# Context weights of tiles 2 and 3 through two free banks, and two wide products ahead of the context sums

## What is computed

```python
scores = jnp.einsum('bhqd,bhkd->bhqk', q, k) / np.sqrt(DK)   # k, v from the 120 context rows
attn = jax.nn.softmax(scores + causal, axis=-1)
out = jnp.einsum('bhqk,bhkd->bhqd', attn, v)
return out @ Wp.T + bp
```

## Time and profile before

| what | value |
|---|---|
| median of 3 runs | 1305.82 us (1305.32 to 1306.38) |
| the profiled execution's own time | 1306.38 us |
| its span in the trace | 1304.6 us |
| period 2, from its first head turn | about 950 to 1070 us |
| period 3 | about 1071 to 1181 us |
| mean granted TensorE clock | 0.947 |

### The profile page before, as it was taken

The page is one execution under the profiler, slowest core; times in us unless marked ns, Lnnn a source line. Parts: engine busy times, 40 slices in busy tenths (PEclk is TensorE's granted clock), DMA queues, the critical chain, the costliest instruction groups (busy, mean ns, idle before and its releaser), DMA issues. The chain is left out here.

```text
span 1304.6 us, 20364 instructions
## 1 busy us (share of the span) xinstructions
PE 1129.9 (87%) x6738; PEld 794.6 (61%) x6738; DVE 744.8 (57%) x2247; ACT 540.8 (41%) x1407; POOL 454.8 (35%) x531
## 2 busy tenths in 40 slices
PE   7889988998898887799999937686998899789996
PEld 3456446545654565799999924452654575466775
DVE  1472476347525835465556528765749576856356
ACT  1371255126422721333333227364465456443541
POOL 0150034004300667566666441525031512222122
PEclk9999999998999997799999958688998999899999
DMA  5000200020001040741111150101000100000000
GB/s 192 17 1 1 56 17 2 1 56 17 1 1 56 2 159 17 262 144 50 50 49 47 40 173 1 33 1 33 1 8 1 33 10 17 1 1 25 1 1 33
DMA packets 40228, 52.38 MB, mean 40 GB/s; under 512 B 10780, under 2 KB 33372, under 8 KB 40124
## 3 DMA queue, kind: packets, MB, share of 16 engines
q1 hardware_dynamic: 31100, 36.66, 8.8%
q0 software_dynamic: 3408, 9.31, 2.6%
q10 hardware_dynamic: 5616, 5.11, 1.2%
HBM read 41.76 MB, written 9.31 MB: 39 GB/s over the span
## 5 line engine op out<-in xcount | busy, mean ns | idle before, releaser
L1327 PE MATMUL bank<-words 128*128 128x256 f32 (+3 forms) x872 | 279.1, 472 | 33.7 <-ACT words L1878 17.4
L1327 PEld LDWEIGHTS bank<-words 128*128 128x128 f32 (+1 forms) x872 | 166.1, 198 | 120.6 <-issue 60.7
L358 PE MATMUL bank<-words 128*128 128x512 f32 x384 | 172.4, 600 | 8.4 <-DMA words<-in_wq 8.4
L324 POOL TENSOR_TENSOR words<-words 128x256 f32<-128x256 f32 (+1 forms) x128 | 103.5, 829 | 192.1 <-DVE words L700 192.1
L886 PEld LDWEIGHTS bank<-words 128*128 128x128 f32 x1248 | 147.7, 195 | 4.2 <-ACT words L920 2.3
L886 PE MATMUL bank<-words 128*128 128x128 f32 x1248 | 148.2, 278 | 1.6 <-ACT words L920 1.6
L571 ACT ACTIVATE words<-words 128x128 f32<-128x128 f32 (+1 forms) x256 | 113.3, 444 | 52.3 <-DVE words L695 52.3
L358 PEld LDWEIGHTS bank<-words 128*128 128x128 f32 x384 | 72.3, 192 | 90.2 <-issue 89.6
L553 ACT ACTIVATE words<-bank 128x512 f32<-128x512 f32 x48 | 28.7, 597 | 191.9 <-PE bank L358 191.9
L935 ACT ACTIVATE words<-words 128x1024 f32 x39 | 41.2, 1057 | 146.5 <-PE bank L886 124.5
L610 DVE COPY words<-bank 128x512 f32<-128x512 f32 x48 | 33.2, 691 | 105.5 <-PE bank L358 105.3
(11 more groups left out here) (300 smaller groups left out, 1991.3 us busy)
## 6 DMA issues: line engine op xcount, KB each, us to landing
words<-in_w SPq DMA_DIRECT2D x8, 1024.0 KB, 12.0
y_slots<-words ACTq DMA_DIRECT2D x39, 128.0 KB, 1.8
words<-in_w SPq DMA_DIRECT2D x8, 512.0 KB, 12.3
words<-in_xt SPq DMA_DIRECT2D x4, 512.0 KB, 4.0
words<-in_x SPq DMA_DIRECT2D x4, 512.0 KB, 4.3
x_rows<-words SPq DMA_DIRECT2D x16, 128.0 KB, 1.8
words<-in_wm SPq DMA_DIRECT2D x2, 1024.0 KB, 6.8
out_x<-words SPq DMA_DIRECT2D x16, 128.0 KB, 1.8
```

The costliest lines, as they stand in the source:

```text
L324: last = pool.tensor_tensor(part, part, inv[:, j % SLOTS0, :, t:t + 1].to_broadcast([P, 2, P * (t + 1)]), ALU.mult)
L358: last = pe.matmul(bank[c % 2][:, :], w, r, start=k == 0, stop=k == KD - 1)
L1327: last = pe.matmul(out, w, r, start=i == 0, stop=i == len(pairs) - 1)
```

## The change

In periods 2 and 3 the turned weights of tiles 2 and 3 go to banks 6 and 7, no longer to bank 1. The fourth `queries_keys`, which uses bank 1, waits for the first two copies alone and stands ahead of those two turns. `up` 0 and 1, which stood between the context sums, stand ahead of all four sums. ACT's order stays; its copies of tiles 2 and 3 read the other banks. The numbers of instructions stay as they were, and period 1 and the closing part issue what they did before.

```diff
@@ tensor, for p in range(1, PERIODS) @@
                 if z is not None:
-                    context_turn(z, 2)
-                    context_turn(z, 3)
-                    pe.wait_ge(xtc, NT * z + NT)
+                    pe.wait_ge(xtc, NT * z + HALF)
                 if a is not None:
                     queries_keys(a, 3)
                 if r is not None:
                     pe.wait_ge(n5.copied, 2 * r + 2)
                 if z is not None:
                     pe.wait_ge(xe, GB * z + GB)
-                for q in range(GB * KD):
-                    if z is not None:
+                    context_turn(z, 2, (6, 7))
+                    context_turn(z, 3, (6, 7))
+                if r is not None:
+                    for c in range(2):
+                        pe.wait_ge(vcop, NT * a + c + 3)
+                        up(r, c)
+                if z is not None:
+                    pe.wait_ge(xtc, NT * z + NT)
+                    for q in range(GB * KD):
                         context_sums(z, q)
-                    if r is not None and q < 2:
-                        if a is not None:
-                            pe.wait_ge(vcop, NT * a + q + 3)
-                        up(r, q)
-                if z is not None:
                     pe.wait_ge(xz, 4 * z + 4)
                     for t in range(NT):
                         context_product(z, t)
@@ scalar @@
                 if z is not None:
-                    context_copy(z, 2)
-                    context_copy(z, 3)
+                    context_copy(z, 2, 6)
+                    context_copy(z, 3, 7)
```

## The result

The changed kernel takes 1301.5 us (median of 11 runs, 1300.02 to 1302.44), and on the same chip the kernel before takes 1305.2 us (11 runs, 1303.3 to 1306.38). The ratio is 0.9974 with a 95% interval of 0.9966 to 0.9983: a gain of 3.7 us. The forecast was 1304.9 us, a gain of 0.9, and a range that began at 1302.0.

A forecast was written before the change was run, and what follows sets the result against it. DVE was taken to bound the edited section, with PE in its shadow. Period 2 wins 0.05 us, period 3 loses 0.9 and wins 1.7, together 0.85 off the 1305.82 median: 1304.9 us, range 1302.0 to 1307.2.

The forecast's parts named there:

- DVE bounds the section, and the adds begin at the clamp: Periods 2 and 3: PE runs in DVE's shadow; first add follows the clamp, 1.58 and 0.33 to 0.64 us earlier.
- The order of PE's work: PE, period 2: projection behind the values, turns in one piece, wide products before sums, 4.7 us hole before product 2.
- Products 2 and 3 at half clock: Context products behind the hole take 1.8 us each; period 2 wins 0.05 us, period 3 loses 0.9.
- The restart of `up` 4: PE before the turn: period 2's 1.8 us clock loss stays, period 3's 1.7 us is won.
- The sum: Periods 2 and 3: 0.05 won, 0.9 lost and 1.7 won, together 0.85 us, giving 1304.9 us.
- both bounds: Periods 2 and 3: adds between +0.85 and -2.2 us; restarts win none of 3.5 us or all of it.
- B: Products 2 and 3 and restarts keep the clock: 1300.1 us, or 1301.8 with adds and one restart; chance 0.17.
- C: Every burst behind a hole pays: products 2 and 3 cold, both restarts slow as before, 1306.7 us; chance 0.14.
- D: Clock stays down through the whole MLP part in both periods: 6.8 us slower, 1312.6 us; chance 0.07.
- E: Nothing moves: products wait for DVE anyway and the adds come when they came, 1305.8 us; chance 0.12.

The follow-up runs named there:

- the second traces: Kernel before, changed kernel and each part of the change alone, rerun unchanged: 1304.37, 1301.67, 1297.95 (turns and projection) and 1302.38 us (wide products).
- the unread product: Kernel before plus one wide product that nobody reads ahead of `up` 4 in periods 2 and 3: 1301.08 us against 1304.45, ratio 0.9974.
- the kernel with one wide product in the hole: Changed kernel with `up` 2 moved between context products 1 and 2, `up` 3 left behind product 3: 1307.98 us against 1308.5 of the kernel before.
- the wide alone: Kernel before with only `up` 0 and 1 moved ahead of the four context sums: 1301.12 us against 1304.45; again, 1302.38 against 1304.37.

## Why the prediction was wrong

*DVE bounds the section, and the adds begin at the clamp.* Right. The section up to the clamp kept its 16.0 us, the first add came 1.25 us behind the start of the clamp in both periods, and ACT did not decide.

*The order of PE's work.* Right. The turns took 1.06 us in one piece, the wide products 3.60, the sums 2.31 and the hole 4.57, where the text had 4.7.

*Products 2 and 3 at half clock.* Right in kind, too dear in size. Period 2 won 0.96 us (7.19 to 6.23) where the text had 0.05, since the clock was still up when product 2 began and fell 0.7 us later, so that DVE waited only for product 3, and for 0.70 us. Period 3 lost 0.64 (6.25 to 6.89) where the text had 0.9. This term was 1.2 us too pessimistic, and the second traces have nearly the same (1.10 won, 0.61 lost).

*The restart of `up` 4.* This is the step that failed. For period 3 the text took the 1.7 us as won, and 1.61 was won. For period 2 it said "a hole of 2.3 after 2.67; I leave the 1.8 us in". It gave no reason why a shorter hole should cost as much as the longer one. The hole was 1.79 us and the restart kept its clock: 1.70 us won where the forecast had none. The hole was misjudged because the term above was: with the wide add 0.9 us sooner, the gelu and `up` 4 came sooner by as much, while PE was done with `up` 3 only 0.4 us sooner than thought. And 1.79 us lies among the holes behind which all 13 restarts kept the clock. That the restart's clock hangs on the work ahead of it is what the unread product shows: with it the hole shrank from 2.67 to 0.95 us and the restart from 5.24 to 3.55 us. Whether a hole of 2.3 us would have cost anything, no run shows; none had a hole between 1.93 and 2.67.

*The sum*: 0.91 + 0.26 at the adds, and 1.70 - 0.09 at the restarts, are 2.78 us over the forecast's 0.85, which gives the 3.63 of the two stretches. The text named both bounds, but gave the low one 17 in 100 and ended the range at half of it. It priced the two restarts apart, one kept slow and one won, though both came out behind holes of nearly one length (1.79 and 1.93 us). The starting point moved too: the 1304.9 was worked out from a median of three runs, 1305.82, and 11 runs gave 1305.2, so 0.6 us of the distance to 1301.5 lies there.

*Rivals.* B, the clock kept, was nearest: 1301.8 with the adds won and one restart, against 1301.5, by another route: both restarts, and 0.3 us at the adds. C, both kinds of burst cold, came true for the context products, which were at half clock from the start in period 3 and from about 0.7 us on in period 2, and not for the restarts. The Trainium skill (page "TensorE: Matmul & The Clock Gate", section "HAM oscillation — how this bites in real kernels") describes a loop whose bursts are shorter than the waits behind them, in which each burst begins throttled. The traces agree in part: products 0 and 1, a burst of 1.99 us ahead of a wait of 4.57, fit that description, and product 2 began throttled in period 3 alone; the restarts, behind a burst of 7.12 us and a wait of 1.79, don't fit it and kept the clock. D, a clock that stays down through the whole MLP part, didn't occur; the nearest to it is the restart of 6.53 us in one period of the kernel with one wide product in the hole. E didn't occur.

*Which part does it.* The turns in two banks with the projection ahead carry the gain: alone they take 5.3 and 6.4 us off. The wide products ahead of the sums, together with them, take some of it back (3.7 us between the two kernels on one chip), and the second traces of both, from that chip, show where. Their spans differ by 2.8 us (1298.8 and 1296.0). Of that 1.2 lies at the adds, nearly all at products 2 and 3 in period 3: behind 4.57 us of hole and not 3.34 they give 6.89 where the turns alone have 5.75. The other 1.7 lies in the closing part (159.9 and 158.2), and nothing at the restarts. In the first trace of the turns alone one restart was slow and the closing part took 159.05, so how steady this split is, two traces of each can't tell.

## What to carry to other kernels

When a section is bounded by another engine, PE's order in it decides little by itself, but it decides where PE stands still, and a long standstill can be paid by the next burst: of the restarts here none paid behind 1.93 us or less, and 11 of 15 behind 2.67 us or more. Look for the burst that everything behind waits for, and keep the wait ahead of it short, if need be with unread work: one product that nobody reads, ahead of each of two such bursts, took 3.4 us off a kernel of 1304.45 us. Filling one hole with work taken from the next one moves the price, and can lose the whole gain.

## What the hardware showed

The position of the clock's fall can be more regular than I had thought. In two traces of the kernel before, whose sections began 1.4 us apart, all four stretches agree within 0.05 us, and in two traces of the change within 0.1. Not in every kernel, though: the turns alone had a restart of 5.23 us in one trace and 3.55 in the other, the wide alone 5.24 and 3.54 in period 3. So it takes more than one trace to tell a habit of a kernel from an accident. And the length of the hole alone doesn't decide: behind 2.67 to 2.99 us the kernel before paid in four restarts of four, and the one with the wide products alone in one of four.
